# A casting transfer for the quantised rows, one norm row on ScalarE and a small step on GpSimd in a state-space layer with an int8 projection

## What is computed

```python
def _layernorm(x, axis=-1, eps=1e-05):
    return (x - mean(x)) / sqrt(var(x) + eps)

# layer 1, state-space scan, 16 states n for each of 512 channels d
xp = x @ x_proj_w.T                      # 64 rank + 16 B + 16 C
delta = softplus(xp[:64] @ dt_proj_w.T + dt_proj_b)
h[t, d, n] = exp(delta * A[d, n]) * h[t-1, d, n] + delta * x * B[t, n]
y[t, d] = sum_n h[t, d, n] * C[t, n] + x * D

# layer 2, each row quantised to int8
x_scale = max(max|x|, 1e-6) / 127
x_q = clip(round(x / x_scale), -128, 127)
out = (x_q @ weight_q.T) * x_scale * weight_scale + bias

x = x + layer1(_layernorm(x));  x = x + layer2(_layernorm(x))
```

## Time and profile before

| | us |
|---|---|
| median of three runs | 2735.76 |
| lowest and highest run | 2733.5, 2736.37 |
| profiled execution, its own time | 2733.05 |
| its span, first to last instruction | 2731.3 |
| busy in the span: PE / PEld | 2703.0 / 2368.5 |
| busy in the span: DVE / ACT / POOL | 2667.9 / 2651.4 / 2641.9 |
| mean granted TensorE clock, share of full | 0.998 |

### The profile page before, as it was taken

The page is one execution under the profiler, slowest core; times in us unless marked ns, Lnnn a source line. Parts: engine busy times, 40 slices in busy tenths (PEclk is TensorE's granted clock), DMA queues, the critical chain, the costliest instruction groups (busy, mean ns, idle before and its releaser), DMA issues.

```text
span 2731.3 us, 80977 instructions
## 1 busy us (share of the span) xinstructions
PE 2703.0 (99%) x33364; PEld 2368.5 (87%) x33364; DVE 2667.9 (98%) x2801; ACT 2651.4 (97%) x5119; POOL 2641.9 (97%) x826
## 2 busy tenths in 40 slices
PE   7999999999999999999999999999999999999998
PEld 6888888888888888888888888888888888888887
DVE  4999999999999999999999999999999999999997
ACT  7899999999999999999999999999999999999995
POOL 4799999999999999999999999999999999999998
PEclk9999999999999999999999999999999999999999
DMA  5355555564554555556655555645556555455443
GB/s 190 100 133 136 144 130 133 139 154 122 146 132 134 142 143 142 125 136 146 148 128 150 134 133 129 158 127 142 128 137 149 136 144 130 133 144 149 126 118 84
DMA packets 337019, 372.68 MB, mean 136 GB/s; under 512 B 227141, under 2 KB 227141, under 8 KB 316298
## 3 DMA queue, kind: packets, MB, share of 16 engines
q1 hardware_dynamic: 315818, 302.48, 38.7%
q0 software_dynamic: 20832, 65.02, 13.5%
HBM read 278.77 MB, written 104.93 MB: 140 GB/s over the span
## 4 chain that ended last, share of the span: by engine, by line
PE 97%; issue 1%; DVE 1%; DMA 0%; POOL 0%; SPq 0%; ACT 0%; DVEq 0%; POOLq 0%
PE PB L835 37%; PE YR L864 21%; PE PB L838 17%; PE YR L859 5%; PE PM L910 4%; PE PM L970 4%; PE PM L929 4%; PE PM L938 2%; PE PM L900 2%; PE PM L917 1%; DVE A L1002 0%; PE PM L881 0%; SPq L467 0%; DMA CB<-c_rows 0%; POOL A L590 0%
## 5 line engine op out<-in xcount | busy, mean ns | idle before, releaser
L590 POOL TENSOR_TENSOR A<-A,CB 128x2048 f32<-128x2048 f32 x511 | 2346.2, 4779 | 47.6 <-ACT CAR L664 47.2
L1002 DVE TENSOR_TENSOR_SCAN A<-A,CAR,PB 128x512 f32<-128x512 f32 x1536 | 1825.4, 1256 | 2.0 <-PE PB L838 1.7
L657 ACT ACTIVATE A<-DEL,an 128x512 f32<-128x512 f32 x2048 | 1340.8, 713 | 4.6 <-PE YR L864 3.5
L835 PEld LDWEIGHTS PB<-DG,XN 128*128 128x128 f32 x8704 | 1043.5, 192 | 112.0 <-issue 84.3
L835 PE MATMUL PB<-DG,XN 128*128 128x128 f32 x8704 | 1100.0, 277 | 8.2 <-DVE A L1002 8.1
L676 ACT ACTIVATE DB<-XN,BC 128x512 f32<-128x512 f32 x960 | 665.8, 714 | 3.6 <-DVE XN L1018 3.4
L864 PE MATMUL YR<-idf,A 64*128 64x64 f32 x16384 | 643.8, 226 | 0.0
L864 PEld LDWEIGHTS YR<-idf,A 64*128 64x128 f32 x16384 | 568.3, 139 | 82.5 <-issue 64.1
L1002 DVE TENSOR_TENSOR_SCAN A<-A,PB 128x512 f32<-128x512 f32 x512 | 585.3, 1201 | 21.5 <-PE PB L838 11.2
L838 PE MATMUL PB<-idf,DB 128*128 128x128 f32 x3840 | 575.8, 279 | 3.2 <-DVE A L1002 2.7
L838 PEld LDWEIGHTS PB<-idf,DB 128*128 128x128 f32 x3840 | 427.7, 141 | 62.4 <-DVE A L1002 13.8
(11 more groups left out here) (96 smaller groups left out, 1559.6 us busy)
## 6 DMA issues: line engine op xcount, KB each, us to landing
CB<-c_rows SPq DMA_DIRECT2D x128, 1024.0 KB, 5.4
DG<-b_diag SPq DMA_DIRECT2D x288, 256.0 KB, 3.5
X<-in_x SPq DMA_DIRECT2D x31, 1024.0 KB, 7.7
out<-X SPq DMA_DIRECT2D x31, 1024.0 KB, 10.2
out<-bias_rows POOLq DMA_DIRECT2D x31, 1024.0 KB, 11.2
out<-C POOLq DMA_DIRECT2D x31, 1024.0 KB, 11.8
b_diag<-DG SPq DMA_DIRECT2D x2, 2304.0 KB, 13.3
b_diag<-BC SPq DMA_DIRECT2D x288, 2.0 KB, 3.0
```

The lines of the kernel that those rows point to most:

```text
L590: gp.tensor_tensor(A[s % NA][:, :, :], A[s % NA][:, :, :], CB[:, s % (4 * NG), :].unsqueeze(1).broadcast_to([128, KB, L]), ALU.mult).then_ ...
L657: act.activation(A[s % NA][:, g, :], DEL[k % 2][:, g, :], ACT.Exp, scale=an[:, g, n:n + 1])\
L835: i = pe.matmul(PB[u % NPB][:, j * 128:(j + 1) * 128], XN[k % 2][:, j, g * 128:(g + 1) * 128], DG[:, (NDG * k + DIAG.index(n)) % NR, j, :] ...
L1002: dve.tensor_tensor_scan(A[s % NA][:, g, :], A[s % NA][:, g, :], PB[(4 * s + g) % NPB][:, :], init, ALU.mult, ALU.add).then_inc(s_scan, 1)
```

## The change

- `xn_p` on POOL does three of the four rows of tiles. The fourth is done by ACT (`xn`): a small 128x1 product of mean and deviation, a wait on itself, and an `Identity` of 128x512 with scale and bias.
- `qt_out` of the chunks before the last goes away. POOL issues a DMA (`cast`) that reads the transposed int16 and writes bf16 into `QT`; `q_mm` waits for its landing.
- `as2` moves from DVE to POOL, as two 128x4 instructions of which the second waits for the first.
- Of twelve groups of eight idle transposes on PE in the first chunk (`warm`) two stay.
- All three tables of places are new.

```diff
-        "as2": (14354,),
+        "as2": (18768,),
+        "cast": (20984,),
-        "turn": (12027,),
+        "turn": (19947,),
...
+    NXP = T - 1
+    NXA = T - NXP
...
+            def as2(p):
+                gp.wait_ge(s_ir, p + 1)
+                gp.tensor_tensor(RO[:, 1, :], PW[:, 1, :], RO[:, 3, :], ALU.mult).then_inc(s_a2, 1)
+                gp.wait_ge(s_a2, p + 1)
+                gp.tensor_tensor(RO[:, 1, :], RO[:, 1, :], RO[:, 2, :], ALU.add).then_inc(s_as, 1)
+
+            def cast(p):
+                if p == END:
+                    return
+                gp.wait_ge(s_tr, 16 * (p + 1))
+                if p >= 1:
+                    gp.wait_ge(s_mm, T * p)
+                gp.dma_start(QT[:, :, :, :].rearrange("p t k l -> p (t k l)"), CT.rearrange("p b r -> p (b r)")).then_inc(s_qd, 16)
...
+            def xn(p, i):
+                j = NXP + i
+                if i == 0:
+                    act.wait_ge(s_rs, p + 1)
+                    if p >= 1:
+                        act.wait_ge(s_xn, NXA * p)
+                act.activation(SM[:, 3, j:j + 1], SM[:, 1, j:j + 1], ACT.Copy, scale=SM[:, 2, j:j + 1]).then_inc(s_sh, 1)
+                act.wait_ge(s_sh, NXA * p + i + 1)
+                act.activation(XN[p % 2][:, j, :].rearrange("p (g r c) -> p g r c", g=KB, r=2),
+                               X[p % NX][:, j, :].rearrange("p (r g c) -> p g r c", g=KB, r=2), ACT.Identity,
+                               bias=SM[:, 3, j:j + 1], scale=SM[:, 2, j:j + 1]).then_inc(s_xn, 1)
...
-                elif j == 0:
-                    act.wait_ge(s_tr, 16 * (p + 1))
-                    if p >= 1:
-                        act.wait_ge(s_mm, T * p)
-                    act.activation(QT[:, :, :, :].rearrange("p t k l -> p (t k l)"), CT.rearrange("p b r -> p (b r)"), ACT.Copy)\
-                       .then_inc(s_qe, 1)
...
                 elif j == 0:
-                    pe.wait_ge(s_qe, p + 1)
+                    pe.wait_ge(s_qd, 16 * (p + 1))
...
-            def as2(p):
-                dve.wait_ge(s_ir, p + 1)
-                for j in range(T):
-                    i = dve.tensor_scalar(RO[:, 1, j:j + 1], PW[:, 1, j:j + 1], RO[:, 3, j:j + 1], RO[:, 2, j:j + 1],
-                                          ALU.mult, ALU.add)
-                i.then_inc(s_as, 1)
```

More of the change, by code:

```diff
@@ L45 @@
+        "q_mm": (20568, 20828, 20985, 21031),
         "q_t": (200000, 200001, 200002, 200003),
[L46 to L49, removed]
+        "qt_out": (200000, 200001, 200002, 200003),
+        "root": (15554,),
+        "rstd0": (-7729,),
+        "scale_a": (20251, 20658, 21028, 21300),
         "scale_out": (200000, 200001, 200002, 200003),
-        "scale_p": (15892,),
-        "scales": (15614,),
@@ L77 @@
-        200011),
-        "weights": (200000, 200001),
[L79 to L82, removed]
+        "scale_p": (21997,),
+        "scales": (15541,),
+        "scan": (412, 412, 412, 440, 541, 687, 853, 890, 1535, 1552, 1582, 1582, 1768, 1974, 2197, 2411, 2411,
[4 rows of a table added]
+        "square": (14968, 14990, 14994, 14998),
+        "step": (18890,),
+        "step2": (19094,),
@@ L83 @@
         "xt_d": (200000, 200001),
-        "xt_out": (-7029, -6748, -6643, -6016),
+        "xt_out": (-6830, -6619, -5829, -5444),
 }
 FIRST = {
[L88 to L95, removed]
@@ new lines @@
+        "add_b": (14306,),
+        "add_c": (22761,),
+        "amax": (12905,),
+        "as2": (18006,),
+        "as4": (14537,),
+        "b_c": (-55650,),
+        "bc_out": (-53117,),
+        "carry": (582, 1247, 1966, 2957, 3792, 4236, 4991, 5367, 6500, 6896, 7677, 8008, 8238, 8920, 9900,
+        10439),
+        "cast": (21070,),
+        "centre": (16420, 16452, 16596, 16962),
+        "d_t": (-54204, -53835, -53479, -53476),
+        "decay": (-1425, -1425, -1371, -900, -182, -12, 700, 750, 773, 925, 1016, 1358, 1412, 1669, 2357, 2357,
[3 rows of a table added]
@@ new lines @@
+        "root": (15375,),
+        "rstd0": (-57934,),
+        "scale_a": (20075, 20528, 20958, 21596),
+        "scale_p": (22626,),
+        "scales": (15293,),
+        "scan": (109, 301, 308, 308, 313, 313, 313, 402, 818, 1567, 3111, 3468, 3551, 3735, 3951, 3952, 4118,
[4 rows of a table added]
+        "square": (12575, 14229, 14532, 14737),
+        "step": (18951,),
+        "step2": (19004,),
+        "store_c": (-61278,),
+        "store_g": (-60227,),
[9 rows of a table added]
+        "times_c": (-77, 1236, 3539, 4426, 4510, 4750, 5317, 5517, 6315, 7019, 7222, 8288, 8705, 8870, 9093,
@@ new lines @@
+        "delta": (-3782, -3474, -3321, -3023),
+        "dl_t": (-1683, -1233, -1070, -154),
+        "du": (-2308, -2276, -2135, -105),
+        "gather": (8871, 10307, 11462, 12820),
+        "idle": (11332, 11378, 11853, 15484),
+        "inv": (14506,),
+        "last_p": (19693, 22210),
+        "last_q": (15126, 15458, 15536, 16553),
+        "last_v": (18536, 20018),
+        "load": (-14381,),
+        "load_c": (1961, 3285, 4708, 5909),
+        "load_g": (-266, 3087, 3528, 3611, 4732, 5113, 5488, 5711, 5804),
@@ new lines @@
+        "log0": (-8200,),
+        "put_last": (10039, 13453, 16977, 17163),
+        "q_mm": (13161, 13577, 14516, 14726),
+        "q_t": (12401, 12662, 13009, 13069),
+        "qt_out": (17248, 18359, 19784, 20321),
+        "root": (16041,),
+        "rstd0": (-7854,),
+        "scale_out": (16607, 16848, 17264, 18405),
+        "scales": (15072,),
+        "scan": (787, 794, 813, 824, 867, 1235, 1253, 1253, 1253, 1255, 1794, 2013, 2578, 2578, 2578, 2578,
[4 rows of a table added]
+        "square": (12926, 14243, 14355, 15570),
@@ L564, in xn_p @@
                                  ALU.add, ALU.mult).then_inc(s_xnp, 1)
-                if p == 0 and i == T - 1:
+                if p == 0 and i == NXP - 1:
                     skip()
@@ L641, in last_p @@
                     gp.tensor_tensor(rows(p)[:, j, :], rows(p)[:, j, :], X[p % NX][:, j, :], ALU.add).then_inc(s_fp, 1)
-            run(bias_p=bias_p, last_p=last_p, step=lambda p, i: step(p), step2=lambda p, i: step2(p), xn_p=xn_p, times_c=times_c, scale_p=lambda p, i: scale_p(p), add_b=lambda p, i: add_b(p), add_c=lambda p, i: add_c(p))
+            run(bias_p=bias_p, last_p=last_p, as2=lambda p, i: as2(p), cast=lambda p, i: cast(p), step=lambda p, i: step(p), step2=lambda p, i: step2(p), xn_p=xn_p, times_c=times_c, scale_p=lambda p, i: scale_p(p), add_b=lambda p, i: add_b(p), add_c=lambda p, i: add_c(p))
         @block.scalar
@@ L1078, in _ @@
             run(last_v=last_v, xt_d=xt_d, gather=gather, du=du,
-                as2=lambda p, i: as2(p), as4=lambda p, i: as4(p),
+                as4=lambda p, i: as4(p),
                 amax=lambda p, i: amax(p),
```

217 lines of the change are left out of this document (93 added, 124 removed), and 96 rows, old and new, of tables (FIRST, LAST, PLACES).

## The result

The changed kernel takes 2879.58 us (median of four runs, 2873.73 to 2883.78) against 2734.86 us for the kernel before: ratio 1.053, 95% interval 1.0518 to 1.0543. The forecast was 2712 us, with a range from 2700 to 2731. The time went up by 145 us where 23 were to be saved.

What follows compares the result with a forecast made beforehand. DVE was taken to set three chunks in four and ACT the fourth, POOL close behind. The span of 2731.3 us less 17.5 for chunks and 6 for the start, plus profiling offsets, gave 2712 us, range 2700 to 2731.

Steps and rivals of the forecast that it cites:

- the part on the transfer: On SP and POOL's cast: moved `turn` leaves later C rows their cover, cast lands in 6 us; costs nothing.
- The part on POOL: POOL's work per chunk: from 82.0 us to 81.95 after the change, at most 82.7.
- the joint at `scale_p`: On POOL: a product between `scale_p` and `add_c` ends a 0.30 us wait, 0.36 us less.
- The slower rival: The cast lands late: past its cover DVE starves one for one; at 17 us landing, 2771 us; chance 0.08.
- the 16.5 of the sum: On DVE: `as2` leaving saves 0.71 us in three chunks of four.
- ACT: Copy of 1.80 us goes, norm pass and small product come: 0.99 us less, about 81.5 us in a sequence's first chunk.
- the upper bound of the sum: POOL's work per chunk at most 82.7 us, with the cast's issue at its dearest.
- the 82.5 that was named as a sign of being wrong: Sign on POOL: the forecast is wrong if POOL's sum per chunk passes 82.5 us.
- the handover at `as2`: Between POOL and DVE: POOL waits some tenths at most; 0.1 us a chunk taken for all handovers.
- Per chunk: DVE sets three chunks at 82.53 us, the fourth takes 82.1: 0.66 us less each, 17.5 us in all after handovers.
- handovers take half: Rival: POOL's waits at `as2`, `centre` or `amax` are passed on, losing 10 us: 2722 us; chance 0.15.
- The start: Fewer idle transposes on PE: first scan near 30.9 us, 5.9 sooner; 6 us saved, bounds 2 and 8.

Runs made afterwards that it cites:

- run 1: Changed kernel with the C rows of states 4 to 7 loaded ahead of the store of X on SP: 2714.36 us, ratio 0.9929 to before.
- run 3: Kernel before, with only the C rows of states 4 to 7 put behind the store and the load of X on SP: 2733.6 us.
- run 8: Mended kernel with the quantised rows copied by ACT again and no cast: 2747.38 us.
- the mended kernel: The kernel of run 1: the changed kernel with its C rows of states 4 to 7 ahead of the store of X, 2714.36 us.
- run 4: Changed kernel, C rows left late, `as2` back on DVE: 2903.7 us. The text has only "a run 4 us under", a time, not this label.
- run 11: Mended kernel with all twelve groups of idle transposes back at the start: 2718.1 us.
- run 6: Changed kernel, C rows left late, with only POOL's issue of `add_c` moved behind the norm and two more products: 2879.13 us.
- run 2: Changed kernel with only the load of X moved behind the C rows, the store of X staying ahead: 2759.88 us.
- run 10: Mended kernel with squares on ACT and `amax`, `inv`, `as4` and `scales` on DVE one scan earlier: 2715.71 us.

## Why the prediction was wrong, point by point

- **The step that failed** is the overlap of the C rows of states 4 to 7, which the sum puts at nothing without looking at it. It stands in the part on the transfer: "the C rows behind it are wanted for the product of state 12 ..., so those loads keep their cover". It followed `turn` past the last C rows, and the sum has no term for anything else that moved on SP. But the new tables also put the store of X, two diagonals and the load of X ahead of the C rows of states 4 to 7. In its place the profile shows POOL waiting for them about 6 us a chunk, and run 1 prices it at 165 us in all. No price stands for that, no rival names it, and the range to 2731 had no room for it. The part on POOL, on the other side, found the norm row and the joint at `scale_p` that make POOL sooner, and counted them as gain only. That they also bring forward the moment at which rows are wanted was not said, nor that the product put into that joint issues `add_c` 4.1 us later and with it moves the burst. The times of run 3 add up to the 5.6 us between it and the changed kernel with these moves; their shares were not tested one by one.
- **The slower rival** had the right form (a transfer lands late, one for one beyond its cover) on the wrong transfer. The cast landed in 8.0 us; 6 was taken, between 3.5 and 11.8, and PE never waited for it. Its issue took 0.61 us to the next start, as taken from `add_b`.
- **DVE**: no `as2` there, and undone it costs 14.2 us against the 16.5 of the sum. **ACT**: right in sign, too small in what a long instruction does there (run 8).
- **POOL**: 81.95 us forecast. In the mended kernel the rows of one chunk give 72.2 for the products, 4.51 for `scale_p`, 0.90 for `add_c`, 2.23 for the norm, 0.61 for the cast, 0.43 and 0.44 for the pairs, all as forecast within 0.03, and 1.34 instead of 0.62 for `add_b`: 82.7, the upper bound of the sum and past the 82.5 that was named as a sign of being wrong. With the median of 1.2 it is 82.5, the period below. The 0.6 to 0.7 us is the handover at `as2`, forecast as "some tenths at most".
- **Per chunk** 0.56 us were to be saved after handovers. The starts of `scale_p` (its first and last, 30 chunks apart) give the periods in the kernel before, the changed and the mended one:

```profile
L610 POOL TENSOR_TENSOR C<-C,wsb x31: 4537/4568/4637, 223.6 to 2709.6; 128x2048 f32<-128x2048 f32 x31
```
```profile
L635 POOL TENSOR_TENSOR C<-C,wsb x31: 4530/4542/4577, 212.5 to 2860.5; 128x2048 f32<-128x2048 f32 x31
```
```profile
L635 POOL TENSOR_TENSOR C<-C,wsb x31: 4520/4555/4571, 210.6 to 2687.0; 128x2048 f32<-128x2048 f32 x31
```

  82.87, 88.27 and 82.55 us. So the mended kernel saves 0.32 a chunk, about 10 us, not 17.5 (and this profile is of a run 4 us under its kernel's median, so it may be a tenth less). That is what the rival "handovers take half" leaves of it.
- **The start** saved more than the 6 us forecast, which makes up the rest. The first scan starts at 30.36 us in the mended kernel (29.75 in the changed one), as forecast (30.9), 6.4 us sooner than at 36.79; but by the first scan of the second chunk the lead is 16.3 us (113.2 against 129.5). The first chunk of the kernel before took 92.7 us, nearly ten more than a later one, and the forecast did not look at that reserve. Two casts of the weights stand in it on DVE: there they take 7.40 and 4.32 us to the next start, in the mended kernel, at other places, 4.88 and 1.51, which is 5.3 of the ten. Why the same cast takes so unequal times is open. By the first `scale_p` 13.0 us of the lead are left (210.6 against 223.6), and with 9.6 us from the thirty periods they make the 22.6 between the two spans. Of the 13.0, run 11 gives 3.7 to the transposes.
- So the mended kernel's 2714.36 us lies by the forecast 2712, but by luck in part: two terms missed by some 7 to 8 us each, in opposite directions.

## What to carry to other kernels

Where tables of places are new, list for each queue every transfer whose neighbours changed, not only the transfer that the change is about, and set its earliest issue against the moment at which its reader wants it. Count what is in flight then: here a load at the end of a burst landed when the burst ended, and a megabyte less ahead of it brought it 3.9 us quicker from POOL's queue (run 6), and 1.6 us sooner and 2.4 quicker from its own (run 2). A step that makes a consumer sooner takes cover from every load that it reads, so speed and cover belong in one sum; and a wait exchanged for another of the same size (run 6) looks in the time like no cause at all until the waits are read.

## What the runs showed of the hardware

- In the chunks shown, the same load of 1 MB of C rows took from issue to landing 14.7 us last in a burst, 10.8 with one megabyte less on another engine's queue, and at most 6.7 when issued 10 us behind the store of X. Over all loads of C rows of the mended kernel the median is 6.0. With all DMA engines busy (0.98 of the time) they moved 301 GB/s.
- A casting DMA, int16 to bf16 within the core's memory, 512 KB: 0.61 us of POOL to issue, 7.5 to 8.3 us to land as the medians of the runs that have it.
- Behind a DMA issue on POOL a 128x2048 product can start after 0.62 us, while the issue's row is 1.39 us long. A 128x4 instruction there starts as soon (0.61, run 10) but takes 0.57 instead of 0.28 us. In the mended kernel it starts only 1.34 us after the issue, 0.07 us behind the `inv` that it needs, and the profile shows no idle time beside the issue's row of 1.28 us.
